# Packing the first chunk of hidden rows, splitting the last one, and moving two element-wise steps of a Macaron layer between engines

## The chip, the cores and the metric

The kernel runs on one core of a Trainium2 chip. The core has TensorE (PE in the profile; PEld is its weight load), VectorE (DVE), ScalarE (ACT), GpSimd (POOL) and SyncE (SP), which here only issues transfers. Each engine works through its own list of instructions and waits for others by semaphores. The metric is the time of one execution on the device in microseconds (us). The kernel before takes 1419.31 us, the median of 3 runs (1419.24 to 1419.68).

## The reference

An input of 2 sequences of 4096 rows with D = 256 columns goes through half a routed feed-forward layer, attention, and the same half feed-forward layer again:

```
def ffn(x):                                      # P = 9 paths, DM = 64
    x_mixed = k[0]*x[s-1] + k[1]*x[s] + k[2]*x[s+1]
    h = einsum('bsd,pdm->bspm', x_mixed, W1) + b1
    paths = einsum('bspm,pmd->bspd', h, W2) + b2
    idx = argmax(tanh(x_mixed @ Wo1 + bo1) @ Wo2 + bo2)
    return layernorm(x + paths[idx], gamma, beta)        # ... * gamma + beta
x = x + 0.5 * ffn(norm(x))
x = x + attention(norm(x))                       # causal, on |scores|
x = x + 0.5 * ffn(norm(x))
```

All is float32 at the interface. The layer norm's shift beta is added after everything else of the feed-forward layer.

## The kernel before, in words

The program is a first feed-forward phase (`ffn(0)`), attention for the two sequences, and a second feed-forward phase (`ffn(1)`). The change touches the two feed-forward phases alone. Each of them goes through 16 tiles of 512 rows; a tile is 4 sub-tiles (u) of 128 rows.

Products of float32 accuracy are made from float16 pairs: a value is a high half and a low half (the rest), and `split_product` (L1821) adds high x high, high x low and low x high, three float16 matmuls. The hidden layer has 640 = 5 x 128 rows: 64 of the router (Wo1) and 9 x 64 of the paths. These are the chunks 0 to 4. In chunk 0 the rows 64 to 127 are path 0; the rows 0 to 63 hold no path, since the router's rows go to the tanh instead, and 9 of them carry the one-hot choice itself, so that b2 is added by the same product. `hidden(t, c)` on TensorE makes a chunk in one of three PSUM banks; VectorE multiplies it by the mask of the chosen path (`masked`, L1002, float32 into `hm`); ScalarE rounds it to float16 (`masked_high`, L1491, into `hhi`), VectorE subtracts (`masked_low`, L1019, into `hlo`), and TensorE's `path(t, c)` (L1936) multiplies by W2. Chunks 0 and 1 are one group of these steps, 2 and 3 the second; chunk 4 (`LAST`, `whole`) isn't split: it is one float32 matmul against `w2_last` for each sub-tile (L1953, in the last tile L1973).

The order is written out by hand as turns, t = 0 to 16, in each engine's `turn(t)`. In turn t TensorE works on `path` of tile t, on chunks 1 to 4 of tile t+1, on the router scores and the one-hot transpose (`choice`) of tile t+2, on chunk 0 of tile t+3 and on the transposes of tile t+5. VectorE begins its turn with `result(t-1)` (L940, which adds the products to the rows); TensorE's `path(t, 0)` waits for it, since both use the same banks. Then VectorE routes tile t+2 (five small steps), mixes the rows of tile t+3 (L851, L859), masks tile t+1, makes the low half of the mixed rows of tile t+3 (`mixed_low`, L863, instruction L866), the low halves of tile t+1 (L1022), scales the result of tile t-1 (L882) and takes the moments of tile t+6. TensorE's `hidden(t+3, 0)`, late in the turn, waits for the low half of the mixed rows.

ScalarE in its turn: tanh and bias of tile t+2 (L1477, L1481), the middle term of the mix (L1434), squares of the result (L1450), the normalised rows of tile t+5 (L1420), the copy of the one-hot choice out of PSUM (L1489), the high half of the mixed rows (`x_high`, L1442), the high halves of tile t+1 (L1497), the copy of the transposes (L1426).

GpSimd in its turn: the inverse root for the result of tile t-1 (L623, L627), the addition of beta to the input rows of tile t (`residual`, L637), the accumulating transfer that adds these rows to the result of tile t-1 (`residual_added`, L647), and the inverse root of the moments of tile t+6 (L604 to L616). `residual` waits until VectorE has masked chunk 0 of the next tile. SyncE's queue sends the one-hot choice to DRAM and spreads it back as masks (`spread`, L465), stores the finished tile and loads a new one.

The last tile of the second phase is done by rows of 128 (`path_by_rows`, L1962; `last_turns`, L961), so that its end can be stored in four pieces.

## Time and profile before

| | |
|---|---|
| median of 3 runs | 1419.31 us |
| the profiled execution's own time | 1418.93 us |
| its span | 1417.1 us |
| mean granted TensorE clock | 0.988 of full speed |
| TensorE busy | 1329.5 us, 94% |
| VectorE busy | 1152.0 us, 81% |
| ScalarE busy | 925.2 us, 65% |
| GpSimd busy | 326.9 us, 23% |
| all transfers | 98.43 MB |

The first feed-forward phase ends near 290 us, the second begins near 1147 us. A busy share says little alone: matmuls are pipelined, the next one begins before the last is over, so for TensorE the distance between starts is what one costs. On VectorE and ScalarE, too, the next instruction begins some 0.1 us before the one ahead is done. The numbers in the timeline's rows are start, duration, engine, line, operation, output <- inputs, and behind them in brackets how long the engine had stood idle and what ended that. "xN" merges N instructions in a row. Every float32 matmul is recorded twice, so "x8" at L1953 is four of them.

### The profile page before, as it was taken

Reading aid. Unit: us, or ns where it says so; the run is one execution under the profiler, and the core shown is the slowest. Engines: PE = TensorE matmul, PEld = TensorE weight load, DVE = VectorE, ACT = ScalarE, POOL = GpSimd, SP = SyncE. Lnnn points to the kernel's source line nnn. Section 1 sums busy time; section 2 is a strip of 40 time slices with the busy share of each in tenths; the row PEclk is TensorE's granted clock in tenths of the full one; section 3 lists DMA queues with packets and bytes.
Section 4 is the critical chain, followed back from the end, with each engine's and each line's share of the span. In section 5 each row is a group of like instructions: output and inputs, shape, how many; then the busy total and the mean of one; then the engine's idle time right before and its main releaser. Section 6 shows DMA issues by size and latency. Waiting matters only on the chain.

```text
span 1417.1 us, 24674 instructions
## 1 busy us (share of the span) xinstructions
PE 1329.5 (94%) x7700; PEld 770.8 (54%) x7700; DVE 1152.0 (81%) x2301; ACT 925.2 (65%) x1717; POOL 326.9 (23%) x396
## 2 busy tenths in 40 slices
PE   4999999988999999998998999999998879999997
PEld 2577776754445454544454455454544346777765
DVE  7899999887778787778877778787778777888876
ACT  6666776465666767565865666767575877766742
POOL 2344553450101000230030101000240003443443
PEclk9999999999999999999999999999999999999999
DMA  6165554440010000102000010000102212555544
GB/s 179 36 168 137 138 150 127 121 120 0 31 46 16 30 30 0 43 3 88 32 22 24 31 46 16 30 30 1 39 7 75 89 33 58 144 143 141 124 110 121
DMA packets 91498, 98.43 MB, mean 69 GB/s; under 512 B 9084, under 2 KB 87429, under 8 KB 91397
## 3 DMA queue, kind: packets, MB, share of 16 engines
q1 hardware_dynamic: 86932, 80.91, 19.3%
q0 software_dynamic: 4464, 16.25, 6.0%
q8 instruction: 54, 0.88, 0.3%
q14 instruction: 48, 0.39, 0.1%
HBM read 55.43 MB, written 25.46 MB: 57 GB/s over the span
## 4 chain that ended last, share of the span: by engine, by line
PE 73%; DVE 15%; ACT 7%; issue 4%; POOL 0%; DMA 0%; DVEq 0%; ACTq 0%; POOLq 0%; SPq 0%
PE PS L1827 64%; PE PS L1953 3%; PE PS L1835 3%; DVE R L1221 2%; DVE R L1215 2%; DVE run_max L1209 2%; PE PS L1924 2%; ACT R L1667 2%; ACT R L1671 1%; DVE x_st L905 1%; ACT R L1626 1%; DVE R L1016 1%; DVE st L816 1%; DVE R L1022 1%; PE PS L1933 1%
## 5 line engine op out<-in xcount | busy, mean ns | idle before, releaser
L1827 PE MATMUL PS<-R 128*128 128x512 f16 (+3 forms) x3456 | 719.9, 363 | 37.3 <-DVE R L1221 27.8
L1827 PEld LDWEIGHTS PS<-R 128*128 128x128 f16 (+1 forms) x3456 | 326.9, 98 | 397.0 <-DVE R L1221 54.9
L1221 DVE TENSOR_TENSOR R<-R 128x512 f16<-128x512 f32 (+3 forms) x288 | 189.2, 657 | 97.2 <-ACT R L1671 95.4
L1658 ACT ACTIVATE R<-PS 128x512 f32 (+5 forms) x288 | 160.4, 558 | 157.2 <-PE PS L1827 157.2
L1667 ACT ACTIVATE R<-R 128x512 f32<-128x512 f32 (+4 forms) x288 | 169.9, 590 | 57.1 <-DVE R L1215 56.3
L1827 PE MATMUL PS<-R,w_hi 128*128 128x512 f16 x636 | 193.5, 386 | 4.6 <-DVE R L866 2.5
L1827 PE MATMUL PS<-w_hi,R 128*128 128x256 f16 x1024 | 188.3, 273 | 3.3 <-DVE R L940 1.5
L1209 DVE TENSOR_TENSOR run_max<-run_max,R 128x512 f32<-128x512 f32 (+3 forms) x272 | 183.0, 673 | 8.4 <-DVE run_max L1209 1.7
L1671 ACT ACTIVATE R<-R 128x512 f16<-128x512 f32 (+3 forms) x288 | 171.7, 596 | 26.9 <-ACT R L1667 0.4
L1215 DVE TENSOR_TENSOR R<-R,max_row 128x512 f32<-128x512 f32 (+4 forms) x288 | 187.3, 650 | 0.5 <-ACT max_row L1735 0.5
L604 POOL TENSOR_SCALAR veps<-mv 128x4 f32<-128x4 f32 x48 | 14.9, 311 | 552.5 <-issue 328.3
L1827 PE MATMUL PS<-w_lo,R 128*128 128x256 f16 x512 | 139.6, 273 | 0.0
L1016 DVE SCALAR_TENSOR_TENSOR R<-PS,b1c,R 128x512 f32<-128x512 f32 x128 | 92.9, 743 | 42.5 <-PE PS L1827 42.5
L1827 PE MATMUL PS<-R,w_lo 128*128 128x512 f16 x318 | 122.5, 385 | 0.0
L1827 PEld LDWEIGHTS PS<-w_hi,R 128*128 128x128 f16 x1024 | 100.2, 98 | 29.9 <-DVE R L940 3.5
L698 POOL TENSOR_TENSOR R<-R 128x1024 f16<-128x1024 f32 x16 | 36.0, 2262 | 288.5 <-ACT R L1633 284.8
L1827 PEld LDWEIGHTS PS<-R,w_hi 128*128 128x128 f16 x636 | 60.5, 103 | 51.7 <-issue 3.6
L1022 DVE TENSOR_TENSOR R<-R 128x1024 f16<-128x1024 f32 x64 | 81.1, 1267 | 0.0
L637 POOL TENSOR_TENSOR R<-R,beta_b 128x1024 f32<-128x1024 f32 x32 | 75.1, 2349 | 3.2 <-DVE R L1013 3.2
L1426 ACT ACTIVATE R<-PS 128x1024 f32<-128x1024 f32 x32 | 32.8, 1025 | 65.6 <-PE PS L1835 65.3
L1420 ACT ACTIVATE R<-R,shift,rstd 128x256 f32<-128x256 f32 x128 | 66.3, 590 | 13.2 <-POOL shift L616 13.2
L1835 PE MATMUL PS<-ident,R 128*128 128x128 f32 x384 | 55.5, 288 | 18.6 <-ACT R L1420 15.8
(137 smaller groups left out, 1698.3 us busy)
## 6 DMA issues: line engine op xcount, KB each, us to landing
R<-x_scratch SPq DMA_DIRECT2D x48, 512.0 KB, 4.4
x_scratch<-R SPq DMA_DIRECT2D x32, 512.0 KB, 3.2
R<-R POOLq DMA_DIRECT2D x31, 512.0 KB, 4.6
R<-oh_scratch SPq DMA_DIRECT2D x32, 320.0 KB
R<-in_L_attn_x SPq DMA_DIRECT2D x16, 512.0 KB, 5.1
R<-oh_scratch SPq DMA_DIRECT2D x32, 256.0 KB
out<-R SPq DMA_DIRECT2D x15, 512.0 KB, 3.1
R<-in_L_ffn_W SPq DMA_DIRECT2D x2, 288.0 KB
```

The costliest lines, as they stand in the source:

```text
L637: g.tensor_tensor(rows4(x_rows(t)), rows4(x_rows(t)), beta_b[:, :].unsqueeze(1).to_broadcast([P, SUB, D]), ALU.add).then_inc(xb_done, 1)
L1016: v.scalar_tensor_tensor(out=at, in0=ps_h[:, h_bank[g, c], :], scalar=b1c[:, c:c + 1], in1=chunk(mask, t, c), op0=ALU.add, op1=ALU.mult).t ...
L1022: v.tensor_tensor(chunk(hlo, t, c, n), masked_chunk(t, c, n), chunk(hhi, t, c, n), ALU.subtract)\
L1209: v.tensor_tensor(run_max[:, lo:], run_max[:, lo:], cols(ring, at, TT - lo), ALU.max)\
L1215: v.tensor_tensor(cols(ring, at, TT - lo), cols(ring, at, TT - lo), max_row[:, lo:], ALU.subtract)\
L1221: v.tensor_tensor(p_lo[:, i * TT + lo:(i + 1) * TT], pf[:, (i % 2) * TT + lo:(i % 2 + 1) * TT], p_hi[:, i * TT + lo:(i + 1) * TT], ALU.sub ...
L1420: ins = a.activation(cols(n_rows(t), u * D, D), cols(x_rows(t), u * D, D), ACT.Identity, bias=shift[:, i, u:u + 1], scale=rstd[:, i, u:u + 1])
L1658: a.activation(cols(ring, ring_m + i * TT + lo, TT - lo), ps_s[:, i, lo:], ACT.Abs, scale=1.0 / (QS * XS * D ** 0.5)).then_inc(abs_done, 1)
L1667: a.activation(p, cols(ring, ring_n + i * TT + lo, TT - lo), ACT.Exp)\
L1671: a.activation(p_hi[:, i * TT + lo:(i + 1) * TT], p, ACT.Copy).then_inc(phi_done, 1)
L1827: ins = t_.matmul(dst, w, xx, start=start and n == 0, stop=stop and n == last, skip_group_check=skip)
L1835: ins = t_.transpose(dst[:, u * P:(u + 1) * P], cols(rows, u * D + c * P, P), ident[:, :])
```

## The change

Four things change in the feed-forward phases.

1. Chunk 0 of the hidden rows uses only 64 + 9 rows. A packed stationary operand is made in `hlo`: its rows 0 to 63 are the low half of path 0 (VectorE, 64 x 512, moved down from rows 64 to 127), its rows 64 to 127 the high half again (a second ScalarE copy). Multiplied by `w2_twice`, which holds path 0's W2 high half twice, it gives high x high and low x high in one matmul; the second matmul is high x low. The one-hot rows are written twice (18 rows in place of 9), and b2 is loaded twice, its high half in the low half's place. So `path(t, 0)` has 2 matmuls for each sub-tile in place of 3. `w2_twice` and this part of `w2_lo` are made once by ScalarE (`pair_weights`).
2. In the second phase chunk 4 is split as the others are: three float16 matmuls in place of one float32 matmul for each sub-tile, one more high half on ScalarE and one more low half on VectorE for each tile.
3. `mixed_low` goes from VectorE's turn to GpSimd's. Before the first turn it stays on VectorE.
4. The addition of beta goes from a GpSimd instruction to an accumulating transfer from GpSimd's queue, whose source is the 256 columns of `beta_b` read four times. It no longer waits for the mask of chunk 0. In ScalarE's turn `x_high` now stands ahead of the one-hot copy.

```diff
     load(w2_v[0:NP, 0, :], b2, w2_in)
+    load(w2_v[NP:2 * NP, 0, :], b2, w2_in)
 def whole(ph, c):
-    return c == LAST
+    return ph == 0 and c == LAST
 # GpSimd
 def residual(t):
     pool.wait_ge(n_done, k + 1)
-    if t < NTT - 1:
-        pool.wait_ge(hm_done, HC * (k + 1) + 1)
-    g.tensor_tensor(rows4(x_rows(t)), rows4(x_rows(t)),
-                    beta_b[:, :].unsqueeze(1).to_broadcast([P, SUB, D]), ALU.add).then_inc(xb_done, 1)
+    if k >= 1:
+        pool.wait_ge(xb_done, 16 * k)
+    g.dma_start(rows4(x_rows(t)), beta_b[:, :].unsqueeze(1).to_broadcast([P, SUB, D]),
+                accum_op=ALU.add).then_inc(xb_done, 16)
+def mixed_low(t):
+    at = use(ph, t) % XBUF * DC * TT
+    pool.wait_ge(xhi_done, use(ph, t) + 1)
+    g.tensor_tensor(cols(xlo, at, DC * TT), xm, cols(xhi, at, DC * TT), ALU.subtract).then_inc(xlo_done, 1)
 def residual_added(t):
-    pool.wait_ge(xb_done, k + 1)
+    pool.wait_ge(xb_done, 16 * (k + 1))
 def turn(t):
     ... result_scale(t - 1)
+    if t >= 0 and mix_on(ph, t + MIX):
+        mixed_low(t + MIX)
     if on(t) and t < NTT - 1:
         residual(t)
 # VectorE
 def route(t, step):    # step 4
-    v.tensor_tensor(oh[:, :, :], r_pr[:, :, :], r_top...to_broadcast([P, SUB, NP]), ALU.is_equal)
+    v.tensor_tensor(oh[:, :, :, :], r_pr...to_broadcast([P, SUB, 2, NP]), r_top..., ALU.is_equal)
 def masked(t, c):      # c == 0
+    if g >= 1:
+        dve.wait_ge(pair_done, g)
 def masked_low(t, i):
+    if c == 0:
+        v.tensor_tensor(chunk(hlo, t, 0)[0:DM, :], masked_chunk(t, 0)[DM:P, :], chunk(hhi, t, 0)[DM:P, :],
+                        ALU.subtract)
+        c, n = 1, n - 1
 def turn(t):
-    if mix:
-        mixed_low(ph, t + MIX)
 # ScalarE
+def pair_weights():
+    a.activation(w2_twice[0:DM, :], w2_hi[DM:P, 0, :], ACT.Copy)
+    a.activation(w2_twice[DM:P, :], w2_hi[DM:P, 0, :], ACT.Copy)
+    a.activation(w2_lo[0:NP, 0, :], w2_hi[0:NP, 0, :], ACT.Copy).then_inc(w2_paired, 1)
 def masked_high(t, i):
+    if i == 0:
+        a.activation(chunk(hlo, t, 0)[DM:P, :], masked_chunk(t, 0)[DM:P, :], ACT.Copy).then_inc(pair_done, 1)
 def turn(t):
+    if mix:
+        x_high(ph, t + MIX)
     if choice:
         one_hot(t + ROUTE)
-    if mix:
-        x_high(ph, t + MIX)
 # before the turns
+    if ph == 1:
+        masked_high(0, 2)
 # TensorE
+def paired_product(dst, high, pair, u, start):
+    t_.matmul(dst, cols(pair, u * P, P), w2_twice[:, :], start=start, stop=False, ...)
+    return t_.matmul(dst, cols(high, u * P, P), w2_lo[:, 0, :], start=False, stop=False, ...)
 def path(t, c):
+    if c == 0:
+        pe.wait_ge(pair_done, g + 1)
```

What the order of the instructions looks like is shown at three places. First GpSimd in a middle turn of the first phase, before:

```order
L623 TENSOR_SCALAR y_var<-y_sq 128x4
L627 TENSOR_TENSOR y_rstd<-y_var,half 128x4
L637 TENSOR_TENSOR R<-R,beta_b 128x1024
L647 DMA R<-R 128x1024
L604 TENSOR_SCALAR veps<-mv 128x4
```

and after:

```order
L627 TENSOR_SCALAR y_var<-y_sq 128x4
L631 TENSOR_TENSOR y_rstd<-y_var,half 128x4
L648 TENSOR_TENSOR R<-R 128x1024
L641 DMA R<-beta_b 128x4x256
L658 DMA R<-R 128x1024
L608 TENSOR_SCALAR veps<-mv 128x4
```

The large GpSimd instruction is now the low half of the mixed rows (L648); beta's addition is a transfer behind it (L641).

Second, ScalarE in a middle turn of the second phase, from the squares to the copy of the transposes, before:

```order
L1450 ACTIVATE R,y_sq<-R 128x256 x4
L1420 ACTIVATE R<-R,shift,rstd 128x256 x4
L1489 ACTIVATE oh_t<-PS 9x512
L1442 ACTIVATE R<-R 128x1024
L1497 ACTIVATE R<-R 128x1024 x2
L1426 ACTIVATE R<-PS 128x2x512
```

and after:

```order
L1469 ACTIVATE R,y_sq<-R 128x256 x4
L1439 ACTIVATE R<-R,shift,rstd 128x256 x4
L1461 ACTIVATE R<-R 128x1024
L1508 ACTIVATE oh_t<-PS 18x512
L1523 ACTIVATE R<-R 128x1024
L1525 ACTIVATE R<-R 64x512
L1523 ACTIVATE R<-R 128x1024
L1523 ACTIVATE R<-R 128x512
L1445 ACTIVATE R<-PS 128x2x512
```

The high half of the mixed rows (now L1461) is ahead of the one-hot copy (L1508); the second copy of path 0 (L1525) and the high half of chunk 4 (the last L1523) are added, both ahead of the copy of the transposes.

Third, VectorE in a middle turn of the second phase, from the masks to the next result, before:

```order
L1013 TENSOR_TENSOR R<-R 128x512
L1016 SCALAR_TENSOR_TENSOR R<-PS,b1c,R 128x512 x3
L866 TENSOR_TENSOR R<-R 128x1024
L1022 TENSOR_TENSOR R<-R 128x1024
L1016 SCALAR_TENSOR_TENSOR R<-PS,b1c,R 128x512
L882 SCALAR_TENSOR_TENSOR R<-R,y_rstd,gamma_b 128x256 x4
L1022 TENSOR_TENSOR R<-R 128x1024
L934 BN_AGGR mv<-x_st 128x2 x4
L940 SCALAR_TENSOR_TENSOR R<-PS,R 128x1024
```

and after:

```order
L1029 TENSOR_TENSOR R<-R 128x512
L1032 SCALAR_TENSOR_TENSOR R<-PS,b1c,R 128x512 x3
L1039 TENSOR_TENSOR R<-R 64x512
L1042 TENSOR_TENSOR R<-R 128x512
L1032 SCALAR_TENSOR_TENSOR R<-PS,b1c,R 128x512
L895 SCALAR_TENSOR_TENSOR R<-R,y_rstd,gamma_b 128x256 x4
L1042 TENSOR_TENSOR R<-R 128x1024
L1042 TENSOR_TENSOR R<-R 128x512
L947 BN_AGGR mv<-x_st 128x2 x4
L953 SCALAR_TENSOR_TENSOR R<-PS,R 128x1024
```

L866 is gone; the first low half is two instructions (L1039, L1042), and behind the masks of chunk 4 there is one low half more. In the first phase that last one isn't there.

## Rows read from the trace of the kernel before

**Rows 1.** Stages: length, PE, PEld, DVE, ACT, POOL busy, PE clock, DMA share, GB/s.

```profile
120.00:160.00 40.00, 40.00 (x273) 28.83 (x272) 37.37 (x81) 27.12 (x55) 18.19 (x21) 1.00 0.56 138
1240.00:1280.00 40.00, 40.00 (x279) 28.26 (x278) 33.53 (x64) 26.42 (x48) 17.10 (x19) 1.00 0.54 142
```

**Rows 2.** Timeline of TensorE: chunk 4 in two turns of each phase.

```profile
155.27 1.89 PE L1953 MATMUL PS<-w_last,R 128*128 128x256 f32 x8
170.82 1.89 PE L1953 MATMUL PS<-w_last,R 128*128 128x256 f32 x8
...
1249.11 1.89 PE L1953 MATMUL PS<-w_last,R 128*128 128x256 f32 x8
1264.66 1.89 PE L1953 MATMUL PS<-w_last,R 128*128 128x256 f32 x8
```

**Rows 3.** Timeline of TensorE in one turn: router, first and last row around path(t, 0).

```profile
1250.83 0.96 PE L1924 MATMUL PS<-wo,th 65*128 65x9 f32 x8
...
1252.94 0.27 PE L1827 MATMUL PS<-w_hi,R 128*128 128x256 f16 x1
...
1254.25 0.59 PE L1827 MATMUL PS<-R,w_hi 128*128 128x512 f16 x2
```

**Rows 4.** Timeline of VectorE in the same turn.

```profile
1258.78 0.75 DVE L1016 SCALAR_TENSOR_TENSOR R<-PS,b1c,R 128x512 f32<-128x512 f32 x1 [1.41 <-PE PS L1827]
1259.44 1.22 DVE L866 TENSOR_TENSOR R<-R 128x1024 f16<-128x1024 f32 x1
...
1266.58 1.22 DVE L940 SCALAR_TENSOR_TENSOR R<-PS,R 128x1024 f32<-128x1024 f32 x1 [1.12 <-PE PS L1953]
```

**Rows 5.** Timeline of ScalarE in the same turn.

```profile
1253.91 2.07 ACT L1420 ACTIVATE R<-R,shift,rstd 128x256 f32<-128x256 f32 x4
...
1258.82 1.99 ACT L1497 ACTIVATE R<-R 128x1024 f16<-128x1024 f32 x2
```

**Rows 6.** Timeline of GpSimd in the same turn; then its low halves in attention (ns: least/median/most).

```profile
1256.22 2.35 POOL L637 TENSOR_TENSOR R<-R,beta_b 128x1024 f32<-128x1024 f32 x1
1264.34 0.94 POOL L647 DMA_DIRECT2D R<-R  x1 [5.76 <-DVE R L882]
...
L698 POOL TENSOR_TENSOR R<-R x16: 2114/2171/2572, 307.1 to 922.1; 128x1024 f16<-128x1024 f32 x16
```

**Rows 7.** Timeline: VectorE's low half beside GpSimd, in each phase's turn 14.

```profile
276.23 2.70 DVE L1022 TENSOR_TENSOR R<-R 128x1024 f16<-128x1024 f32 x1
...
1394.85 2.73 DVE L1022 TENSOR_TENSOR R<-R 128x1024 f16<-128x1024 f32 x1
...
1391.84 4.66 POOL L637 TENSOR_TENSOR R<-R,beta_b 128x1024 f32<-128x1024 f32 x2
```

**Rows 8.** Timeline of TensorE in turns 12 and 13 of the first phase.

```profile
238.16 0.28 PE L1827 MATMUL PS<-w_hi,R 128*128 128x256 f16 x1 [0.70 <-DVE R L940]
...
253.82 0.28 PE L1827 MATMUL PS<-w_hi,R 128*128 128x256 f16 x1 [0.38 <-DVE R L940]
```

**Rows 9.** Timeline: before the first turn of the second phase.

```profile
1171.50 0.74 DVE L1016 SCALAR_TENSOR_TENSOR R<-PS,b1c,R 128x512 f32<-128x512 f32 x1
...
1171.07 1.00 ACT L1426 ACTIVATE R<-PS 128x1024 f32<-128x1024 f32 x1
...
1172.98 1.06 PE L1924 MATMUL PS<-wo,th 65*128 65x9 f32 x8 [0.77 <-ACT th L1477]
```

**Rows 10.** Timeline of TensorE and VectorE in turns 14 and 15 of the second phase.

```profile
1388.76 0.28 PE L1827 MATMUL PS<-w_hi,R 128*128 128x256 f16 x1 [0.43 <-DVE R L940]
...
1401.07 0.27 PE L1827 MATMUL PS<-w_hi,R 128*128 128x256 f16 x1 [1.28 <-issue]
...
1399.75 1.22 DVE L1022 TENSOR_TENSOR R<-R 128x1024 f16<-128x1024 f32 x1
```

**Rows 11.** Page: GpSimd's queue and its accumulating transfers.

```profile
q0 software_dynamic: 4464, 16.25, 6.0%
...
R<-R POOLq DMA_DIRECT2D x31, 512.0 KB, 4.6
```

56 lines of the change are left out of this document (38 added, 18 removed).

## The prediction

> **What bounds the kernel now.** I read the stages first: in a stretch of either feed-forward phase TensorE is busy without a gap (40.00 of 40 us) at the full clock (1.00, so 2.4 GHz), VectorE 37.4 us in the first phase and 33.5 us in the second, ScalarE 27 to 28 us, GpSimd 17 to 18 us, the transfer engines 0.54 to 0.56 [rows 1]. So a shorter list on TensorE can be worth its full price there, and VectorE is the next engine. Then TensorE's timeline: chunk 4 of one tile stands 15.55 us behind that of the tile before, in both phases, to the hundredth [rows 2]. So steady a distance over 10 turns in each phase is an engine that waits for nobody. Then VectorE in such a turn: it waits 1.41 us for a hidden chunk and 1.12 us for the end of the products [rows 4]. Its waits reset it twice a turn, so small additions to it cost nothing until they exceed these. Last the places where TensorE does wait: turns 12 and 13 of the first phase, the start and the end of the second.
>
> The price of a matmul is the distance of starts, not its duration. `path(t, 0)` has 12 float16 matmuls of 256 columns from 1252.94 to 1254.25 [rows 3]: 1.31 us, 0.109 each. Chunk 4's four float32 ones go from 1249.11 [rows 2] to 1250.83 [rows 3]: 1.72 us, 0.43 each.
>
> **The change part by part.** All sums are made against the profiled execution's own time, 1418.93 us (1.83 us outside its span of 1417.1); the median shown is 0.38 us more.
>
> *Packed chunk 0, TensorE.* 8 matmuls in place of 12: 4 x 0.109 = 0.44 us for each tile. I take a matmul with the packed operand at the price of the others, since rows and columns are the same; a bound below would be none saved in a moving operand that is new (w2_twice), above 0.44. First phase: 16 x 0.44 = 7.0 us. The turn should be 15.11 us.
>
> *Split chunk 4, TensorE, second phase.* 12 x 0.109 = 1.31 in place of 1.72 us: 0.41 us a tile. The turn should be 15.55 - 0.44 - 0.41 = 14.70 us. Up to the end of tile 13 it pays: 14 x 0.44 = 6.1 us and 13 x 0.41 = 5.3 us, 11.4 us in all; the last two tiles I count separately below.
>
> *VectorE.* Goes: L866, after which the next begins 1.13 us later (its row says 1.22 [rows 4]). Comes: the first low half in two pieces, 0.61 x 2 in place of 1.13, so 0.1 us; a one-hot of twice the width, under 0.1 us; in the second phase a low half of 512 columns, 0.6 us. I take the 512-column price as half of L1022's 1.13 and a little start. First phase: 37.4 / 40 x 15.55 = 14.5 us of work, now 13.6 in a turn of 15.11. Second: 13.0, now 12.7 in 14.70. It stays behind TensorE. Order matters more than the sum: from the masks of chunk 4 on, which wait for TensorE at about 9.9 us of a turn, VectorE has 0.66 + 1.6 + 1.13 + 0.6 + 0.3 us to do in the second phase and is at the next result at 14.3, TensorE's products end at 14.7, and `path(t, 0)` wants the result only 2.1 us into the next turn. Hidden by 0.4 us, and by 0.7 us more in TensorE's head start.
>
> *ScalarE.* Adds a 64 x 512 and, in the second phase, a 128 x 512 copy, 0.6 us each by half of L1497 (0.95 from start to start) and a start [rows 5]. 28.6 / 40 x 15.55 = 11.1 us becomes 12.3 of 14.70. `x_high` moved ahead of the one-hot copy begins when the normalised rows are done, at 1255.98 [rows 5], 5.1 us into the turn (the turn begins at 1250.83), and ends at 6.1. The one-hot copy stood at 6.5 before and follows at once, so SyncE's mask transfers go no later. Cover: the masks are wanted in the next turn only.
>
> *GpSimd.* `mixed_low` there is 2.17 us, at most 2.57, by the same shape in attention [rows 6]; it waits for `x_high` and runs from 6.2 to 8.4 us of the turn. TensorE asks for it at about 12 us. What is queued behind it: beta's transfer, then `residual_added`, which waits for VectorE's scaled result at about 12.2 us anyway, then the inverse root for a later tile. L637, 2.35 us, goes from the same place (1256.22 is 5.4 us into the turn). So GpSimd's large instruction is exchanged for one of its size. Issuing beta's transfer: the other accumulating transfer holds GpSimd 0.94 us [rows 6]; the new one has four pieces of 1 KB for each partition in place of one of 4 KB, so between 0.94 and 4 x 0.94 = 3.8 us. I take 1 to 2; even 3.8 us ends at 12.2. Both are hidden. Its landing: 4.6 us by the other one [rows 11]; it is wanted a turn later.
>
> *The lock between VectorE and GpSimd.* In each phase's turn 14 two L637 in a row run beside a low half of VectorE, which then takes 2.70 and 2.73 us in place of 1.22 [rows 7]; it ends just when they do. The Trainium skill, page "SBUF — State Buffer", section "Who interferes with whom", states that a VectorE instruction with both inputs in SBUF and a GpSimd instruction that reads SBUF exclude each other for the whole instruction; by that rule, the trace agrees, and moving `mixed_low` to GpSimd sets up a new meeting. Where it runs now, VectorE has masks that read PSUM and then waits for TensorE until about 7.5 us (7.95 before, less 0.44; 1258.78 [rows 4]); its first low half comes at 8.2 us, so the meeting is some 0.2 us. I take nothing.
>
> *End of the first phase.* In turns 12 and 13 TensorE waits 0.70 and 0.38 us for VectorE's result [rows 8], 0.9 and 0.5 us by the starts around them. VectorE is saturated there by the sums of the first keys; without L866 it is earlier by more than a microsecond a turn. 1.3 us come back. In turn 14 the locked low half (2.70) becomes 1.3: 1.4 us on the chain to tile 15's products, of which the two tiles' 0.87 are counted, so 0.5 us. First phase together 7.0 + 1.8 = 8.8 us.
>
> *Start of the phases.* In the second, TensorE's first router product waits 0.77 us for ScalarE's tanh [rows 9], behind the copy of the transposes. Ahead of that copy now stand the second copy (0.55) and chunk 4's high half, which needs the masks of chunk 4, done at 1172.2 (1171.50 [rows 9] and 0.1 for the split). So the copy begins at 1172.9 in place of 1171.1 and route(2) comes at 1174.6 in place of 1173.0: a loss of 1.6 us, from 0 (if ScalarE can be earlier) to 1.8. In the first phase ScalarE stands idle for 1.4 us between the two high halves, and the three copies of pair_weights and the pair copy (1.6 us) go there: 0 to 0.2.
>
> *End of the second phase.* In turn 14 `path(14, 0)` waits for VectorE (0.43 us, 1388.76 [rows 10]); VectorE's list ahead of that result is 0.6 us longer now, TensorE's is shorter, so it comes 0.5 us later against the hidden chunk that starts it. Then the lock goes (2.73 to 1.3, of which 0.8 counts, since the masks of chunk 4 then wait for TensorE), and a low half of 0.6 and a masked wait come in ahead of the last tile's products, which waited for L1022 at 1399.75 and started at 1401.07 [rows 10]. Worked through in order, the products of the last tile start 11.5 us behind `path(14, 0)` in place of 12.3, and the tail behind them, which hangs on VectorE, ScalarE and GpSimd by turns, keeps its length: 0.75 us gained.
>
> **The sum.** 8.8 + (11.4 - 1.6 - 0.5 + 0.75 = 10.1) = 18.9 us. 1418.93 - 18.9 = 1400.0; as a median 1400.4 us, 1.3% less. Attention isn't touched and should only be shifted. Its first steps run beside GpSimd's low halves; a different meeting there can give or take 2 us.
>
> **The rivals.**
>
> *A. The lock holds VectorE in each turn.* If GpSimd's low half began with VectorE's first one (at 8.2 us, not 6.2), that would wait 2.2 us. The room is 0.4 us ahead of chunk 4's masks, 0.4 behind in the second phase (0 in the first) and 0.7 in TensorE's head start: 1.1 us lost in a turn of the first phase, 0.7 in one of the second, over 10 and 12 turns 19 us, so no gain at all: 1419. Half of it, 1409, if the meeting is partly avoided. For: [rows 7]. Against: ScalarE is free for `x_high` at 5.1 us.
>
> *B. Beta's transfer is late at the end.* In the last turns two of them follow each other, the second waiting for the first to land, and VectorE's last rows need the second. At 4.6 us it is there 2 us ahead; at 8 us, plus 2 more for issuing, it costs about 4 us: 1404.
>
> *C. The accumulating transfer is paid by the piece: slower.* The place is the 16 transfer engines in every turn. 6.0% of the span is 85 us for 31 transfers [rows 11], 2.7 us each over 16 engines, 0.34 us for each 4 KB piece (8 to an engine). If a piece of 1 KB cost the same 0.34, 32 pieces to an engine are 10.9 us a transfer; with 0.55 x 15.55 = 8.6 us of load there now the turn would be 19.5 us, 4 us over the old one, and 28 turns of it make 1418.93 + 110 = 1530. It decides from (15.55 - 8.6) / 32 = 0.22 us a piece; by bytes it is 0.085, which I take. The Trainium skill, page "DMA: Bandwidth & Descriptors", section "Why small descriptors are slow (HBM only)", says that transfers inside SBUF don't suffer from small pieces; no run here shows it for accumulating ones.
>
> *D. The packed matmuls save nothing that counts*, because another engine takes TensorE's place at 15.5 us: VectorE would have to be 1.5 us slower than worked out. 1417 to 1420.
>
> **How the numbers follow.** Forecast 0.72, with its own range 1397 to 1403. A 0.10 (half of it faster than 1414), B 0.09, C 0.04, D 0.03, and 0.02 for a larger gain, since waits of turns that I didn't follow might go too. The range 1397 to 1408 leaves out about 0.16. Within 0.2% (2.8 us, about what a measurement can tell here) of 1419.3 lie D and a part of A: 0.04. Slower by more: C and the worst of A, 0.05. Faster 0.91.
>
> **What would show it.** From one tile's chunk 4 to the next 15.11 us in the first phase and 14.70 in the second; L1971/L1972 (the packed products) 8 starts in 0.87 us. `mixed_low` on GpSimd (L648) from 6 to 8.5 us of the turn, and VectorE's L1039 and L1042 at 0.7 and 1.2 us: durations of 2 us and more there are rival A. The waits of 0.70 and 0.38 us gone. The transfer engines' share up by 0.15 to 0.2: near 1 would be C. The first router product of turn 0 of the second phase 1.6 us later against its hidden chunk. It would be wrong if the turns come out at other lengths than these two, or if attention changes its length.

## The result and the profile after

The changed kernel takes 1410.97 us (median of 4 runs, 1408.43 to 1411.51) against 1419.30 us: a ratio of 0.9937 (0.9925 to 0.995). In a later series of five it took 1409.51 us, ratio 0.9927 (0.9914 to 0.9941). It is faster, by 8.3 us and not by 18.9. Its profiled execution took 1411.25 us.

From the page after (engine busy times; the mean busy share of the transfer engines in 40 slices; GpSimd's queue with packets, MB and share; its transfers with the median from issue to landing):

```profile
span 1409.5 us, 24682 instructions
PE 1313.0 (93%) x7636; PEld 752.4 (53%) x7636; DVE 1141.1 (81%) x2323; ACT 957.3 (68%) x1768; POOL 353.6 (25%) x422
DMA  6288788840010000102010010000002212888876
q0 software_dynamic: 21360, 33.03, 14.7%
R<-beta_b POOLq DMA_DIRECT2D x32, 512.0 KB, 6.4
R<-R POOLq DMA_DIRECT2D x31, 512.0 KB, 6.9
```

The same two stages as in [rows 1], with their columns:

```profile
120.00:160.00 40.00, 40.00 (x271) 28.58 (x270) 36.69 (x85) 30.68 (x61) 23.85 (x25) 1.00 0.85 179
1240.00:1280.00 40.00, 40.00 (x293) 28.27 (x291) 35.25 (x75) 32.18 (x64) 23.40 (x25) 1.00 0.90 195
```

TensorE has 16.5 us less to do in the whole span. The transfer engines are busy at 0.85 and 0.90 in the stages, where they were at 0.56 and 0.54 before [rows 1], and the residual's transfer lands after 6.9 us, not 4.6 [rows 11].

The steady turns are what was forecast. TensorE's router products of two neighbouring turns of each phase, and the first and last of the eight packed matmuls of a turn:

```profile
154.84 0.96 PE L1956 MATMUL PS<-wo,th 65*128 65x9 f32 x8
169.95 0.96 PE L1956 MATMUL PS<-wo,th 65*128 65x9 f32 x8
...
1232.59 0.96 PE L1956 MATMUL PS<-wo,th 65*128 65x9 f32 x8
1234.69 0.27 PE L1971 MATMUL PS<-w_twice,R 128*128 128x256 f16 x1
...
1235.46 0.27 PE L1972 MATMUL PS<-w_lo,R 128*128 128x256 f16 x1
1247.29 0.96 PE L1956 MATMUL PS<-wo,th 65*128 65x9 f32 x8
```

15.11 us and 14.70 us; packed matmuls start 0.11 us apart, the price taken from [rows 3].

So what is missing lies outside the ordinary turns. This table cuts both traces at the starts of router products (L1924, now L1956; the start of their weight load) and of VectorE's result of tile 15 (L940, now L953):

| stretch | before | after | difference | forecast |
|---|---|---|---|---|
| start to the router product of turn 0 | 48.04 | 48.92 | +0.88 | 0 |
| first phase, turn 0 to turn 13 | 202.92 | 197.02 | -5.90 | -7.0 |
| turn 13 to the result of tile 15 | 37.79 | 38.18 | +0.39 | -1.8 |
| attention, to the first router product behind it | 860.30 | 862.15 | +1.85 | 0 |
| start of the second phase, three router distances | 39.37 | 42.11 | +2.74 | +0.75 |
| second phase, 12 turns | 184.85 | 175.67 | -9.18 | -10.2 |
| turn 13 to the end | 43.83 | 45.41 | +1.58 | -0.65 |
| sum | 1417.1 | 1409.5 | -7.65 | -18.9 |

**The end of the first phase.** SyncE's queue (issue, duration, line; L492 is the store of a tile, L526 a load, L476 the one-hot store of 18 KB, L481 the first mask transfer, which waits for that store to land), VectorE's first mask of the last tile, and the same store and mask transfer before (9 KB there, since the one-hot rows stood once):

```profile
251.57 0.41 SPq L492 DMA_DIRECT2D x_scratch<-R  x1
252.02 1.43 SPq L526 DMA_DIRECT2D R<-x_scratch  x1
253.55 0.41 SPq L476 DMA_DIRECT2D oh_scratch<-oh_t  x1
259.84 0.58 SPq L481 DMA_DIRECT2D R<-oh_scratch  x1
```

```profile
266.32 0.69 DVE L1029 TENSOR_TENSOR R<-R 128x512 f32<-128x512 f32 x1 [2.17 <-DMA R<-oh_scratch]
```

```profile
258.88 0.29 SPq L472 DMA_DIRECT2D oh_scratch<-oh_t  x1
261.92 0.58 SPq L477 DMA_DIRECT2D R<-oh_scratch  x1
```

From the issue of the one-hot store to that of the mask transfer that waits for its landing it is 6.3 us; in the same turn before it was 3.0 us. (I measure the landing this way throughout.) The masks come late, and VectorE stands still for 2.17 us. The doubled size isn't the cause: in this turn (13) the store takes 2.9 to 3.8 us in all five traces without beta's transfer, of which e1 and e2 have the 18 KB, and 5.3 to 6.4 us in all seven that have beta's transfer and the store on SyncE's queue, of which e3 has the 9 KB. Earlier, in turn 12, TensorE still waits 0.44 us for VectorE's result, of the 0.70 in [rows 8]; the 0.38 of turn 13 is gone. (This second wait lies behind the router product of turn 13, so some 0.5 us of the forecast's 7.0 in the table belong one row lower.)

```profile
233.56 0.28 PE L1971 MATMUL PS<-w_twice,R 128*128 128x256 f16 x1 [0.44 <-DVE R L953]
```

**One turn of the second phase** takes 15.72 us, not 14.70. VectorE's and GpSimd's rows in it:

```profile
1327.65 2.04 DVE L1029 TENSOR_TENSOR R<-R 128x512 f32<-128x512 f32 x1 [2.24 <-DMA R<-oh_scratch]
```

```profile
1327.02 2.12 POOL L648 TENSOR_TENSOR R<-R 128x1024 f16<-128x1024 f32 x1 [0.71 <-ACT R L1461]
```

Late masks again; and VectorE, 2.24 us behind its place, now meets GpSimd's low half, and its masking takes 2.04 us in place of 0.69: it ends 0.55 us behind GpSimd's instruction. The second trace of the changed kernel (e12) has no longer turn here, though VectorE waits there too, for 1.46 and 1.57 us. In an ordinary turn the two miss each other, as the prediction said:

```profile
161.16 2.13 POOL L648 TENSOR_TENSOR R<-R 128x1024 f16<-128x1024 f32 x1
163.23 1.37 POOL L641 DMA_DIRECT2D R<-beta_b  x1
```

```profile
163.13 0.70 DVE L1039 TENSOR_TENSOR R<-R 64x512 f16<-64x512 f32 x1
163.85 0.69 DVE L1042 TENSOR_TENSOR R<-R 128x512 f16<-128x512 f32 x1
```

**The clock.** Stretches of both traces (columns as in [rows 1]; the clock is the number before the last two), first after, then before, near the border between attention's two sequences:

```profile
742.00:750.00 8.00, 7.12 (x22) 2.46 (x20) 5.42 (x15) 4.04 (x9) 0.00 (x0) 0.57 0.00 0
```

```profile
743.00:751.00 8.00, 4.13 (x21) 1.60 (x19) 7.74 (x13) 4.23 (x10) 1.41 (x1) 1.00 0.40 130
```

Behind the same gap of 2.6 us in TensorE's work the clock falls to 1.2 GHz after and not before: 2.4 us. At the start of attention it was low for 3.4 us less: 0.6 back. Then the start of the second phase, TensorE's router product of turn 0 and the stretch behind it:

```profile
1172.02 1.33 PE L1956 MATMUL PS<-wo,th 65*128 65x9 f32 x8 [2.41 <-ACT th L1496]
```

```profile
1172.00:1176.00 4.00, 3.98 (x16) 2.26 (x17) 2.61 (x8) 3.68 (x7) 1.72 (x4) 0.58 0.08 16
```

The wait was 0.77 us before [rows 9]; now it is 2.41, and the clock falls behind it, where it was full before (the stretch of the same length from the router product on, before):

```profile
1173.00:1177.00 4.00, 4.00 (x29) 2.91 (x30) 3.43 (x13) 2.94 (x5) 1.89 (x4) 1.00 0.39 102
```

That costs 1.7 us. All 17 traces fit this: where the router product of turn 0 comes 10.1 to 10.4 us behind the one before it (nine traces), the clock is at 1.2 GHz behind the wait; where it comes 8.2 to 8.8 us behind (eight traces), it stays at 2.4 GHz there.

**The tail**, from the chain of waits (start, us, what):

```profile
1382.65 6.96 DMA R<-beta_b
...
1390.17 0.72 POOL R L641
1390.90 7.89 DMA R<-R
```

GpSimd waits until beta's transfer for tile 14 has landed before it issues that for tile 15, and everything behind it, the residual of tile 14 among it, waits in line.

### The profile page after: what moved, and what is told of

Its sections match the earlier page's. It is cut to its first block, busy times and chain, and to the rows that moved or that the text cites. A ratio compares the mean times of both kernels' runs of the same rounds, so it can differ in the third digit from the quotient of the medians.

```text
span 1409.5 us, 24682 instructions
## 1 busy us (share of the span) xinstructions
PE 1313.0 (93%) x7636; PEld 752.4 (53%) x7636; DVE 1141.1 (81%) x2323; ACT 957.3 (68%) x1768; POOL 353.6 (25%) x422
## 4 chain that ended last, share of the span: by engine, by line
PE 67%; DVE 14%; ACT 7%; issue 6%; DMA 4%; POOL 1%; SPq 0%; DVEq 0%; ACTq 0%; POOLq 0%
PE PS L1859 59%; DVE R L1240 3%; PE PS L1867 2%; DVE R L1234 2%; DVE run_max L1228 2%; ACT R L1699 2%; PE PS L1956 2%; DMA R<-R 2%; ACT R L1703 2%; PE PS L1994 1%; DVE x_st L918 1%; ACT R L1658 1%; DMA R<-oh_scratch 1%; DMA oh_scratch<-oh_t 1%; PE PS L1971 1%
## 5 line engine op out<-in xcount | busy, mean ns | idle before, releaser
L1859 PE MATMUL PS<-w_hi,R 128*128 128x256 f16 x896 | 164.6, 273 | 2.6 <-DVE R L1042 2.6
L1859 PE MATMUL PS<-w_lo,R 128*128 128x256 f16 x448 | 122.2, 273 | 0.0
L1523 ACT ACTIVATE R<-R 128x1024 f16<-128x1024 f32 (+1 forms) x80 | 77.2, 965 | 35.3 <-DVE R L1032 34.7
L1859 PEld LDWEIGHTS PS<-w_hi,R 128*128 128x128 f16 x896 | 87.5, 98 | 24.1 <-DVE R L1042 2.8
L1042 DVE TENSOR_TENSOR R<-R 128x512 f16<-128x512 f32 (+1 forms) x80 | 70.7, 900 | 0.4
L1469 ACT ACTIVATE R<-R 128x256 bf16<-128x256 f32 x124 | 49.9, 404 | 22.7 <-DVE R L953 22.6
```

The source lines that it names most:

```text
L1042: v.tensor_tensor(chunk(hlo, t, c, n), masked_chunk(t, c, n), chunk(hhi, t, c, n), ALU.subtract)\
L1523: a.activation(chunk(hhi, t, c, n), masked_chunk(t, c, n), ACT.Copy).then_inc(hhi_done, 1)
L1859: ins = t_.matmul(dst, w, xx, start=start and n == 0, stop=stop and n == last, skip_group_check=skip)
```

## The experiments

Fifteen runs, two of them (e12, e15) of the two kernels again. I call the parts of the change P (packed chunk 0, split chunk 4), B (beta by transfer) and L (low half by GpSimd). ScalarE's new order comes with P and with L; no run has it alone. Executions of one kernel differ by 1.4 to 6 us. The runs e1 to e4 were made on one chip, e5 to e8 and e13 to e15 on a second, e9 to e12 on a third; each ratio is against the kernel before on the same chip.

**e1, the changed kernel without B.**

```diff
-                    g.dma_start(rows4(x_rows(t)), beta_b[:, :].unsqueeze(1).to_broadcast([P, SUB, D]),
-                                accum_op=ALU.add).then_inc(xb_done, 16)
+                    g.tensor_tensor(rows4(x_rows(t)), rows4(x_rows(t)),
+                                    beta_b[:, :].unsqueeze(1).to_broadcast([P, SUB, D]), ALU.add).then_inc(xb_done, 1)
```

> The changed kernel with one part undone: beta is added by the GpSimd instruction again, the packed chunk 0, the split chunk 4 and GpSimd's low half stay. Theory Q (the changed kernel, at 1411.0, lost time because beta's transfers fill the queues: the one-hot store lands after up to 6 us, VectorE waits for masks in turn 14 of the first phase and turn 11 of the second, 1.2 and 1.0 us on the path, and the last rows wait for beta's second transfer, 2 us): those waits go, 4.2 us, and the lock of the two additions in turn 14 comes back, 0.5 us a phase: 1407.8. Theory L (the lock between VectorE and GpSimd): GpSimd now has two large instructions in a row, from 6.2 to 10.8 us of the turn, beside VectorE's first low half at 8.2; that one waits 2.3 us a turn, of which 1.1 us is not covered in the first phase and 0.7 in the second: 1407.8 plus 19, about 1427. Between them 1415.

1438.02 us, ratio 1.013 (1.0114 to 1.0145): theory L, and stronger than the 1427 us written. Turns are 16.62 and 15.66 us, 1.5 and 1.0 us over the changed kernel's where 1.1 and 0.7 were expected. GpSimd, then VectorE in one:

```profile
172.12 2.13 POOL L648 TENSOR_TENSOR R<-R 128x1024 f16<-128x1024 f32 x1
174.21 2.82 POOL L641 TENSOR_TENSOR R<-R,beta_b 128x1024 f32<-128x1024 f32 x1
```

```profile
173.64 1.17 DVE L1039 TENSOR_TENSOR R<-R 64x512 f16<-64x512 f32 x1
174.82 2.76 DVE L1042 TENSOR_TENSOR R<-R 128x512 f16<-128x512 f32 x1
```

VectorE's two pieces take 3.9 us in place of 1.4. The first ends 0.56 us behind GpSimd's low half, the second 0.55 us behind its addition: each waits until GpSimd's instruction is over and then runs. The Trainium skill, page "SBUF — State Buffer", section "Who interferes with whom", says that the ports which VectorE and GpSimd share are an exclusive lock, and that a VectorE instruction with two inputs in SBUF contends with a GpSimd instruction that reads SBUF; by that rule, the trace agrees.

Theory Q has its part as well: VectorE never waits for masks in this trace, nor in those of e2, e14 and the kernel before (both), which all do without beta's transfer. Each of the twelve traces with beta's transfer has at least one such wait.

**e2, P alone.** The kernel before with the packed and split chunks and ScalarE's new order; in the code of e1 the line of GpSimd's low half goes and VectorE's comes back:

```diff
+                    if mix:
+                        mixed_low(ph, t + MIX)
```

> The kernel before with TensorE's part alone: packed chunk 0, split chunk 4 in the second phase. Beta by GpSimd and the mixed rows' low half by VectorE as before, ScalarE's order as in the changed kernel. Theory Q: the turns are 15.11 and 14.70 us, since VectorE has 14.6 us of work in the first and 13.8 in the second; no transfer was added, so no wait for masks; the waits for VectorE's result in turns 12 and 13 grow from 1.1 to about 2 us: 1419.3 - 7.0 - 11.4 + 1.6 + 1 + 1 = 1404.5, faster than the whole change. Rival V (VectorE becomes the bound without GpSimd's help): turns of 15.3 and 14.9 us, 1410 or later.

1420.42 us, ratio 1.0006 (0.9997 to 1.0015): nothing gained, rival V. The turns are 15.88 and 14.92 us; in the first phase TensorE waits for VectorE's result (waits from 60 to 210 us: sum, times, longest). VectorE and GpSimd meet here too:

```profile
PE PS L1971 <- DVE R L951: 4.7, 8, 0.6
```

```profile
167.10 1.98 DVE L877 TENSOR_TENSOR R<-R 128x1024 f16<-128x1024 f32 x1
```

```profile
165.64 2.35 POOL L641 TENSOR_TENSOR R<-R,beta_b 128x1024 f32<-128x1024 f32 x1
```

With TensorE's products done sooner, VectorE reaches its low half sooner and runs into GpSimd's addition, which before had ended 0.55 us ahead of VectorE's arrival (162.71 + 2.34 against 165.60). A turn 0.33 us longer than the old one is what the shorter list on TensorE gives.

**e3, B alone.** In the kernel before, the edit of e1 the other way round.

> The kernel before with beta by transfer alone. Theory Q: TensorE sets the turn at 15.55 us, which gives the masks 0.4 to 0.85 us more time than in the changed kernel, so at most one turn has a wait for masks (0 to 1 us); the lock in both turns 14 goes (0.5 us each), the last rows wait for beta's second transfer (2 us): 1419.3 + 1 = 1420.5. Rival (beta's transfer costs nothing): 1418.3.

1418.99 us, ratio 0.9998 (0.9989 to 1.0007). Turns of 15.55 us, and one wait for masks, 0.73 us in turn 14 of the first phase, as theory Q allows. The 2 us that it gives to the last rows aren't seen: from turn 13 to the end it is 44.06 us, 43.84 before. The two theories lay too close together for the time to tell them apart.

**e14, L alone.**

```diff
-                    if mix:
-                        mixed_low(ph, t + MIX)
...
+                    if t >= 0 and mix_on(ph, t + MIX):
+                        mixed_low(t + MIX)
```

> The kernel before with one part alone: the mixed rows' low half by GpSimd (with ScalarE's high half ahead of the one-hot copy). GpSimd then has two large instructions in a row, its own low half and the addition of beta, beside VectorE's low halves. Theory L (the lock): as in e1, whose turn was 16.62 us with a VectorE list 0.1 us longer, VectorE waits some 2.5 us a turn; its list is 1.13 us shorter than before and it had 2.5 us of waits for TensorE: the turn becomes 16.3 to 16.5 in the first phase and 15.55 to 15.6 in the second: 1419 + 10 x 0.9 = 1428. Rival (no lock, VectorE relieved): turns of 15.55, 1418.

1425.31 us, ratio 1.0035 (1.0022 to 1.0049), with ScalarE's new order: the lock, with turns of 15.83 in the first phase and 15.55 in the second; less than I wrote.

**e8, P and B without L.** The edit of e2 in the changed kernel.

> The changed kernel with one part undone: the low half of the mixed rows is VectorE's again; packed and split chunks and beta by transfer stay. In e2_tensor_part VectorE set the turn (15.88 and 14.91 us), and 0.76 us of that is the lock: its low half of the mixed rows took 1.98 us in place of 1.22 beside GpSimd's addition of beta. Theory K (beta's transfer helps by taking that lock away): the turn is 15.88 - 0.76 = 15.12 us, TensorE's own, in the first phase and 14.70 in the second, so VectorE doesn't need GpSimd's help in steady turns, and the kernel is at 1411 to 1413, with some waits in turns 11 to 14 of the first phase. Rival G (VectorE needs to be rid of the low half): 15.8 and 14.9, 1418 to 1420.

1408.96 us, ratio 0.9924 (0.991 to 0.9938): theory K. Turns of 15.12 and 14.70. Without L the one-hot store lands sooner: in turns 5 to 9 of the first phase after 1.4 to 1.9 us, with L after 3.7 to 4.6. The residual's transfer, too, lands after 4.7 us here and 4.6 in e3, but after 6.9 in the changed kernel: it comes late only where B and L meet.

| parts | us | turns |
|---|---|---|
| none | 1419.3 | 15.55, 15.55 |
| P | 1420.4 | 15.88, 14.92 |
| B | 1419.0 | 15.55, 15.55 |
| L | 1425.3 | 15.83, 15.55 |
| P, L | 1438.0 | 16.62, 15.66 |
| P, B | 1409.0 | 15.12, 14.70 |
| P, B, L | 1411.0, 1409.5 | 15.11, 14.70 |

No part alone gains. P is paid only once B has taken GpSimd's large instruction away, and L adds nothing that these times show.

**e4, the tail.** A semaphore of its own for the last tile of a phase.

```diff
-                    if k >= 1:
-                        pool.wait_ge(xb_done, 16 * k)
+                    if t < NTT - 1 and beta_before(k):
+                        pool.wait_ge(xb_done, beta_before(k))
...
+                                accum_op=ALU.add).then_inc(xb_last if t == NTT - 1 else xb_done, 16)
```

> The changed kernel with one wait taken away: beta's transfer for the last tile of each phase has a semaphore of its own, so it is issued behind that of the tile before and doesn't wait for its landing. Theory W (the tail hangs on GpSimd's wait in order: issue 1382.7, landing 1389.6, second issue, landing 1398.8): the second transfer lands about 5 us earlier and the span ends as the rows of the tile do, 2 us earlier: 1409.0. Theory Q, the queues themselves: both transfers share the same 16 engines and the residual's transfer is queued behind them, so at most 0.5 us: 1410.5 to 1411.

1407.59 us, ratio 0.9917 (0.9904 to 0.9931). The stretch from turn 13 to the end is 43.41 us in place of 45.41 (44.44 in e12, the second trace of the changed kernel): theory W, 1 to 2 us.

**e5, start of the second phase**, on e4. ScalarE's order:

```diff
                 masked_high(0, 0)
-                masked_high(0, 1)
-                if ph == 1:
-                    masked_high(0, 2)
+                if ph == 0:
+                    masked_high(0, 1)
                 transposed(ph, 4)
```

and in turn 0 of the second phase both high halves behind `scores`.

> The kernel of e4_tail_apart (1407.6) with ScalarE's order at the start of the second phase changed: the copy of the transposes and the tanh of the router stand ahead of the high halves of chunks 2 to 4, so TensorE's router product of turn 0 doesn't wait for these. Theory C (a longer wait of TensorE brings the lower clock): in the changed kernel TensorE waits 2.41 us for that tanh (0.77 before) and then runs at 1.2 GHz for 3.4 us, where it ran at 2.4 before; the wait falls to about 0.8 us and the low clock behind it isn't there: 1.6 + 1.7 = 3.3 us, 1404.3. Rival (the low clock comes at its own time, whatever the wait): at most 1.6 us, 1406.0, and the rows still show 1.2 GHz there.

1407.07 us, ratio 0.9909 (0.9895 to 0.9923): no change that can be told from e4. The first wait is 0.77 us as expected, but two others came for it, and the low clock, too, only moved (1191.1 to 1194.5 us):

```profile
1178.85 0.39 PE L1978 MATMUL PS<-ident,oh 128*18 128x128 f16 x4 [1.26 <-DVE oh L1023]
...
1189.25 1.06 PE L1969 MATMUL PS<-wo,th 65*128 65x9 f32 x8 [1.22 <-ACT th L1507]
```

VectorE now waited for the postponed high halves, so the one-hot, the moments of tile 5 and all behind them came later. Neither theory is settled by it.

**e6, the masks**, on e4. The one-hot store goes from SyncE's list to ScalarE's, behind the copy.

```diff
+                    act.wait_ge(ohT_done, g + 1)
+                    if g >= 2:
+                        act.wait_ge(mask_in[g % 2], 16 * MASK_LOADS * (g // 2))
+                    a.dma_start(oh_d[t % 2], oh_t[:, :]).then_inc(oh_stored, 16)
```

> The kernel of e4_tail_apart (1407.6) with the store of the one-hot issued by ScalarE right behind its copy, not by SyncE. Theory F (SyncE's queue: the store of 18 KB stands behind the 1 MB of the tile's store and the next load, landing after 3.7 to 6.3 us; masks come late in single turns by chance): on a queue of its own it lands in about 2 to 3 us, the waits of VectorE for masks (3.8 us in the profile of e4) go, and the median falls by 0 to 1 us: 1407.0. Rival E (the 16 engines themselves are full with beta's pieces): it lands as late as before, the same waits: 1407.6 or later by what ScalarE pays for the issue.

1404.83 us, ratio 0.9899 (0.9881 to 0.9917), by the medians more than I gave it, though the interval overlaps e4's. In the turn shown above, ScalarE's and SyncE's issues, and the same two in e10, which has this edit too:

```profile
253.01 0.27 ACTq L1519 DMA_DIRECT2D oh_scratch<-oh_t  x1
```

```profile
256.39 0.58 SPq L481 DMA_DIRECT2D R<-oh_scratch  x1
```

```profile
254.03 0.27 ACTq L1518 DMA_DIRECT2D oh_scratch<-oh_t  x1
259.66 0.58 SPq L481 DMA_DIRECT2D R<-oh_scratch  x1
```

3.4 us in place of 6.3, with the store and the load ahead of it as in the changed kernel. But e10's 5.6 us, and 5.5 in e13, show that a queue of its own doesn't secure this: beta's transfer, issued some 1.4 us ahead, still holds the engines. What is seen each time is the shorter stretch. VectorE doesn't wait in e6; from turn 13 to the result of tile 15 it is 35.84 us in place of 38.18, 1.95 less than in the kernel before: the forecast had 1.8. All four traces with this edit and with L have 35.8 to 36.1 us there, the five of changed kernels with the store on SyncE's queue 37.3 to 40.3. The Trainium skill, page "DMA: Bandwidth & Descriptors", section "Queues, rings and completion order", says that a transfer engine takes turns between queues; by that rule, e6's trace agrees, and e10's and e13's show how little it can give. e6's tail is 45.08 us, see e9.

**e7, pieces of 2 KB**, on e4: beta stands twice in its row (one load more; to make room, the routing's `r_pr` shares `r_eq`'s buffer).

```diff
-                    g.dma_start(rows4(x_rows(t)), beta_b[:, :].unsqueeze(1).to_broadcast([P, SUB, D]),
+                    g.dma_start(x_rows(t).rearrange("p (u d) -> p u d", u=2), beta_b[:, :].unsqueeze(1).to_broadcast([P, 2, 2 * D]),
```

> The kernel of e4_tail_apart (1407.6) with beta's transfer in pieces of 2 KB in place of 1 KB (beta stands twice in its row). Worked out from the traces, 32 transfers of 512 pieces of 1 KB add 14.7% x 1409.5 - 6.0% x 1417.1 = 122 us for each of the 16 engines, 0.119 us a piece; the residual's pieces of 4 KB take 0.34, 0.085 per KB. Theory P (a part of a piece's price is fixed, 0.04 to 0.05 us): a 2 KB piece takes 0.2 us, the share of that queue falls from 14.7 to about 12.8%, masks and landings come earlier by about 0.6 us, the time by 0 to 0.7: 1407.2. Rival (price by bytes, the rest is crowding): the share stays at 14.7 and the time at 1407.6.

```profile
q0 software_dynamic: 13168, 33.03, 13.5%
```

13.5% of 1406.3 less the residual's 85 us is 105 us for 512 pieces on each engine: 0.205 us for 2 KB against 0.119 for 1 KB. A line through the two has a fixed 0.033 and 0.086 per KB: theory P, smaller than written. It isn't a law: it would give 0.38 us for 4 KB, where the residual's pieces take 0.34 [rows 11], and with the same sum other traces give 0.109 us (e9) and 0.115 (e3) for 1 KB and 0.192 (e11) for 2 KB. The time, 1408.27 us, ratio 0.9921 (0.9907 to 0.9935), doesn't show it.

**e9, beta behind the one-hot store**, on e6.

```diff
+                    if on(t + ROUTE):
+                        pool.wait_ge(oh_stored, 16 * (use(ph, t + ROUTE) + 1))
```

> The kernel of e6_onehot_own_queue (1404.8) with one wait more: GpSimd issues beta's transfer only when the one-hot store of the same turn has landed. In e6 and e4 the store lands 1.4 us after its issue in steady turns of the second phase, where GpSimd's low half keeps beta's transfer behind it; in turn 13, which has no low half, beta's transfer goes 2 us ahead of the store, that lands after 5 us, and VectorE waits 4.2 us (2.6 in e4) for the masks of the last tile. Theory Q (which transfer is first in the 16 engines decides): the last masks go at about 1366 and not 1369.8, VectorE's wait there is under 1.5 us, the tail is 43.4 us in place of 45.1: 1402.8. Rival (the order doesn't matter, the engines hold so much in turn 13 anyway): 1404.8, wait of VectorE over 2.5 us.

The place is as theory Q has it (tail 43.41 us, no wait for the last masks), the time isn't: 1404.73 us, ratio 0.9893 (0.9878 to 0.9908). Nor does the tail speak for this edit: e10, without it and with a wait of 2.22 us for the last masks, has 43.42 us. What stands out is e6's one trace, with a wait of 4.18 us. And the 1.4 us that I gave for the store's landing in steady turns of e6's second phase were wrong; the trace has 2.6 to 5.0 us in turns 2 to 9. What the edit does is at the end of the first phase: with beta's transfer behind it the store there lands after 3.2 us (3.0 in e11). In the first phase the masks now share the engines with beta's transfer, and one turn had a wait of 2.4 us.

**e10, the start again**, on e6: tile 0 of the second phase keeps chunk 4 whole, VectorE's moments go ahead of a low half, one high half goes behind the tanh.

```diff
-            return ph == 0 and c == LAST
+            return k <= NTT and c == LAST
...
+                    input_moments(5)
                     masked_low(0, 1)
-                    masked_low(0, 2)
-                    input_moments(5)
```

> The kernel of e6_onehot_own_queue (1404.8) with the start of the second phase changed: chunk 4 of its first tile stays whole in float32, VectorE takes the moments of tile 5 before the low half of chunks 2 and 3, ScalarE makes the high half of these behind the router's tanh. Theory C (each wait of TensorE there costs, and brings the lower clock in the turn after it): the three first router distances, 10.5 and 16.4 us in e6, become 8.9 and 15.1 to 15.4, waits under 0.8 us each, no stretch at 1.2 GHz between 1169 and 1195: 2.5 us less, 1402.3. Rival (the low clock comes whatever the wait): 8.9 and 16.8, 1404 to 1405.

1401.66 us (1401.01 to 1404.55), ratio 0.9872 (0.9857 to 0.9887): the fastest, ahead of both kernels; its interval still overlaps e6's a little. TensorE's waits, and the stretch behind the first:

```profile
1169.05 1.06 PE L1967 MATMUL PS<-wo,th 65*128 65x9 f32 x8 [0.97 <-ACT th L1502]
...
1175.30 0.39 PE L1976 MATMUL PS<-ident,oh 128*18 128x128 f16 x4 [0.40 <-DVE oh L1019]
```

```profile
1169.00:1173.00 4.00, 3.95 (x27) 2.67 (x28) 2.18 (x5) 3.83 (x6) 2.69 (x4) 1.00 0.37 98
```

The three router distances are 39.89 us, in place of 42.11 in the changed kernel and 41.12 in e6, and the clock stays up, as theory C says. The trace, of the slowest of the four executions (1404.55 us), shows 1.2 us of the 2.5 expected here.

**e11, all together**: e7, e9 and e10 on e6.

> All that helped in one: beta's last transfer on its own semaphore and in pieces of 2 KB, the one-hot store on ScalarE's queue, beta behind that store's landing, the start of the second phase as in e10. If the gains add: 1404.8 - 2.0 - 2.5 = 1400.3. If the clock gives the start of the phase back: 1402.5. The granted clock at the border of attention's two parts alone can move a run by 2.4 us.

1403.97 us, ratio 0.9896 (0.988 to 0.9911): the gains don't add; no better than e10.

**e12, the changed kernel again; e15, the kernel before again** (one execution).

> The changed kernel itself once more, for a second trace and beside the others. Steady turns are 15.11 and 14.70 us again by every theory. Theory X (which stretches of attention are at 1.2 GHz differs from execution to execution, from 896.3 to 901.2 us for the same instructions): attention is another length than 900.3 in this trace or in the spread of the runs, 1407 to 1412. Rival (it belongs to the changed kernel): 900.3 again. VectorE's late masks (turn 14 of the first phase, turn 11 of the second): the first again, since the order of the transfers there is fixed, the second perhaps not.

> The kernel before once more, one look. Turns of 15.55 us. Theory X (position of the stretches at 1.2 GHz is a matter of the execution): its attention takes between 896 and 903 us, not necessarily 898.1 again, and its third router product stands between 48.0 and 49.5 us, as in the other kernels. Rival: 898.1 and 48.0 again.

From turn 13's router product to the next phase's first e12 takes 902.91 us, where the first trace had 900.34. But 2.1 us of the difference are the end of the first phase, with its late masks (40.29 us against 38.18); attention itself, from the result of tile 15 on, takes 862.62 against 862.15 us. In the kernel before it takes 860.35 in e15 and 860.30 in the first trace. So theory X isn't borne out for attention: each kernel repeats its own within 0.5 us. It is for the start: e15 has 49.01 us up to turn 0, where the first trace had 48.04, and e12 49.35 against 48.92. So the 0.88 us lost at the start are no more than two traces of one kernel differ by.

Over all 17 traces attention itself takes 861.6 to 863.1 us in the nine that have 1.2 GHz for 6.8 us near the border of its two sequences, and 859.6 to 860.4 us in the eight that have it there for 3.4 us or not at all. Which kernel is in which group follows no single part of the change: e4 is in the first, e7, which differs from it in the pieces of beta's transfer, in the second.

e12 had late masks as well, one of them in a first-phase turn with the lock behind it:

```profile
101.32 2.47 DVE L1029 TENSOR_TENSOR R<-R 128x512 f32<-128x512 f32 x1 [1.83 <-DMA R<-oh_scratch]
```

```profile
101.12 2.13 POOL L648 TENSOR_TENSOR R<-R 128x1024 f16<-128x1024 f32 x1 [0.73 <-ACT R L1461]
```

**e13, VectorE's low half back**, the edit of e2 on e10.

> The kernel of e10_start_by_order (1401.7) with the mixed rows' low half by VectorE again. Theory K (once beta's addition is a transfer, no lock is left and VectorE has time for it: in the first phase 14.9 us of work in 15.11, in the second 14.0 in 14.70): turns of 15.11 and 14.70, VectorE's result in turns 12 and 13 and the result of turn 14 later by 1 to 2 us (e8: first results of the end 1.1 us later than in the changed kernel), 1402.5 to 1403.5. Rival G (needed): VectorE-bound turns of 15.3 and more, 1406.

1404.26 us, ratio 0.9897 (0.9882 to 0.9912): turns of 15.12 and 14.70, theory K. By its trace 0.7 us are lost in turn 12 to 13 of the first phase. In e10's company L is worth up to 2.6 us, with intervals that overlap by a little.

## Why the prediction was wrong

The direction, the steady turns and the first wait of the second phase were right, the size wasn't: 8.3 us of 18.9. The step that cost most is the one on the mask transfers. By its own steps:

- *Packed chunk 0 and split chunk 4.* Right to the hundredth: 15.11 and 14.70 us.
- *VectorE "stays behind TensorE".* Right for the whole change. But VectorE's list was summed as if the lock were a matter of turn 14. e2 shows that it is met in each turn as soon as TensorE is faster. That B hides in this sum as a condition was not seen.
- *"SyncE's mask transfers go no later".* This step failed. It asked when the one-hot store is issued, which is right (6.9 us into an ordinary turn, 7.2 before), not when it lands: 6.3 us later in place of 3.0 in turn 13 of the first phase, for the masks of turn 14, behind a store, a load and beta's pieces, and only in traces with beta's transfer. It cost 2.2 us at the end of the first phase (e6: 1.95 gained where I wrote 1.8) and 1.0 in the second, the lock included; in e12 these 1.0 are not there, but 1.6 us in turns 3 and 4 of the first.
- *End of the first phase, 1.3 us of waits.* TensorE still waits 0.44 of 0.70 us, and the 0.38 are gone; about half came back.
- *Start of the second phase, 1.6 us.* The wait itself cost 1.8, but the clock fell behind it, another 1.7 (e10: both nearly gone).
- *End of the second phase.* Rival B, taken at 0.09 and priced at about 4 us, is what happened besides, at 1 to 2 us (e4 against the two traces of the changed kernel).
- *Attention "only shifted", with 2 us either way.* +1.85, by the clock and not by GpSimd's low halves: 2.4 us lost at the border of the sequences less 0.6 regained at the start. The granted clock differs at both places, and the distance between the two traces changes for good nowhere else in attention.
- *Start of the first phase.* +0.9 is the difference of two traces of one kernel (e15): chance, as far as the runs tell.
- *Rival A.* It doesn't hold in an ordinary turn of the changed kernel, but in those with late masks, and in full in e1, e2 and e14. The lock was read too mildly from [rows 7]: VectorE's low halves don't end just when GpSimd's instructions do, but 1.08 us behind (278.93 against 277.85, 1397.58 against 1396.50), which is the time they need by themselves. *Rival C* is refuted: 0.119 us a piece where it needed 0.22, though not the 0.085 I took; so accumulating transfers in small pieces cost more for the same bytes here than in large ones. The transfer engines' share rose by 0.29 and 0.36, not by 0.15 to 0.2.

The missing 11.2 us by the two traces: 2.2 + 1.0 masks, 2.2 tail, 0.3 + 1.7 start of the second phase, 1.85 attention, 0.9 start, 1.1 waits of the first phase. e10's trace takes back the first three groups. That the parts sum up is by construction; which cause goes with which part is shown by runs for the masks, the tail and the wait at the start, and by where the clock differs for the rest.

Open: why the clock stays low for 6.8 us near the border of attention's sequences in some kernels and not in others; what ScalarE's order does alone; the single late turns of e9 and e12; and the rest of the spread between executions of one kernel.

## What to carry over

A transfer that is hidden by its own duration can still move others: follow each small store that something waits for, by its landing, and look which large transfer is issued just ahead of it, on any queue. A queue of its own helped here but did not secure the landing; the large transfer behind it did in two traces, and showed no gain in time. When the bounding engine gets faster, the others meet at new places: redraw the whole turn, shared ports included, before the gain is booked, since here no part gained alone and two together, P and B, gained as much as all three. Where the bounding engine waits longer than before, add the lower clock that may follow the wait to its price, and where a phase ends, look for transfers that wait for each other on one semaphore.

## What the hardware showed that I had not expected

- An accumulating transfer inside SBUF costs 0.109 to 0.119 us for a piece of 1 KB, 0.192 to 0.205 us for 2 KB and 0.34 us for 4 KB on its engine.
- A store of 9 or 18 KB behind 1 MB on SyncE's queue lands after 2.9 to 3.8 us, and after 5.3 to 6.4 us when 512 KB more have just been issued on GpSimd's. From ScalarE's queue it then takes 3.4, 5.5 and 5.6 us in three traces, and 3.0 to 3.2 us when the 512 KB are issued behind it.
- TensorE is at 1.2 GHz for 3.4 us behind a wait of 2.41 us, and at 2.4 GHz behind waits of 0.77 and 0.97 at the same place.
- Attention, with the same instructions, took 859.6 to 860.4 us in eight traces and 861.6 to 863.1 in nine, which show more of it at 1.2 GHz. A forecast of less than half a per cent on this kernel has to know that.
